# Attention starts straight from the projections; router, expert weights and expert tiles go between its turns

## The reference, cut to what matters

```
xn  = layernorm(x)
q, k, v = xn@Wq * mod, xn@Wk * mod, xn@Wv      # 16 heads of width 8, mod = cos(phase)*amplitude
s   = q@k.T / sqrt(8) * cos(2*pi*(i-j)/2048)   # per head, 2048 x 2048
w   = softmax(s);  w = (w + roll(w, 1)) / sqrt(2)
att = (w@v) * mod, all heads side by side, @ Wo
# experts: 8, each token takes its two best
logits = small per-token attention of xn@wqkv.T (8x8, with its own exp)
top two logits -> two experts and two weights (softmax of the two)
he  = (silu(xn@w1[e,:352].T) * (xn@w1[e,352:].T)) @ w2[e].T
out = x + att + sum over the two experts of weight*he
```

## Time and profile before

| | us |
|---|---|
| median of 3 runs | 709.84 (708.99 to 710.26) |
| the profiled execution | 707.88 |
| its span, first to last instruction | 706.1 |
| attention, first score matmul to last value matmul | about 206.8 to 692.0 |
| mean granted TensorE clock | 0.962 |

### The profile page before, as it was taken

One profiled execution on the slowest core, in us unless ns is written; L12 is line 12 of the kernel. 1 busy time (PEld: TensorE's weight loads), 2 busy tenths in 40 slices (PEclk: granted clock), 3 DMA queues, 4 the chain that ended last, 5 costly groups with the idle time before them and its releaser, 6 DMA issues.

```text
span 706.1 us, 11470 instructions
## 1 busy us (share of the span) xinstructions
PE 621.4 (88%) x4151; PEld 201.4 (29%) x4152; DVE 220.7 (31%) x462; ACT 550.1 (78%) x530; POOL 93.3 (13%) x109
## 2 busy tenths in 40 slices
PE   3984057999989999999999999999999999999995
PEld 3841034677751111111111111111111111111113
DVE  7578024334420031423233142331414232005003
ACT  1466024233358999999999999999999999999992
POOL 2038720111110101010010101101010000000000
PEclk9998568899998999999999999999999999999999
DMA  4934321111141101011010101101010010000002
GB/s 129 313 121 148 120 62 66 45 45 59 48 131 47 43 5 46 16 31 36 12 46 1 47 16 31 43 3 46 1 46 25 19 35 1 3 1 1 1 0 63
DMA packets 33828, 34.44 MB, mean 49 GB/s; under 512 B 6092, under 2 KB 27878, under 8 KB 33650
## 3 DMA queue, kind: packets, MB, share of 16 engines
q1 hardware_dynamic: 30786, 27.01, 13.3%
q0 software_dynamic: 2992, 6.76, 2.9%
HBM read 21.14 MB, written 12.58 MB: 48 GB/s over the span
## 4 chain that ended last, share of the span: by engine, by line
PE 60%; ACT 18%; issue 13%; DVE 7%; SPq 2%; DMA 0%; ACTq 0%; DVEq 0%
PE ps L1098 23%; ACT big L581 16%; PE ps L1081 15%; PE ps L981 4%; PE ps L974 4%; PE ps L986 3%; DVE m L771 2%; PE ps L964 2%; SPq L339 2%; PE ps L1116 2%; PE ps L1105 1%; PE ps L915 1%; PE ps L906 1%; DVE big L717 1%; PE ps L959 1%
## 5 line engine op out<-in xcount | busy, mean ns | idle before, releaser
L581 ACT ACTIVATE big<-ps 128x1536 f32<-128x1536 f32 x342 | 471.2, 1459 | 11.9 <-PE ps L1081 4.5
L1098 PE MATMUL ps<-big,vh 128*32 128x512 f32 x2048 | 274.1, 607 | 0.1
L1081 PE MATMUL ps<-qa,ka 49*128 49x512 f16 x896 | 179.8, 385 | 12.2 <-ACT big L581 9.2
L771 DVE TENSOR_REDUCE m<-ps 128x1 f32<-128x512 f32 x128 | 88.5, 692 | 157.5 <-PE ps L1116 157.5
L1081 PEld LDWEIGHTS ps<-qa,ka 49*128 49x128 f16 x896 | 33.1, 93 | 227.1 <-ACT big L581 157.1
L1098 PEld LDWEIGHTS ps<-big,vh 128*32 128x32 f32 x2048 | 40.4, 108 | 103.8 <-issue 98.2
L436 POOL COPY vh<-vaug 128x144 f32 x16 | 5.1, 319 | 382.1 <-PE ps L1098 380.8
L1116 PE MATMUL ps<-ka,attnT 49*128 49x512 f16 x128 | 48.0, 375 | 6.0 <-DVE m L771 5.7
L755 DVE COPY osb<-ps 128x512 f32<-128x512 f32 x16 | 11.1, 692 | 126.7 <-PE ps L1098 126.7
L738 DVE TENSOR_TENSOR cs<-pair,ps 128x352 f32<-128x352 f32 x39 | 20.3, 521 | 85.2 <-PE ps L986 81.6
L553 ACT COPY y<-ps 128x128 f32<-128x128 f32 x39 | 10.4, 266 | 45.6 <-PE ps L974 45.6
(11 more groups left out here) (165 smaller groups left out, 370.9 us busy)
## 6 DMA issues: line engine op xcount, KB each, us to landing
qk_parts<-store SPq DMA_DIRECT2D x16, 256.0 KB
qa<-qk_parts SPq DMA_DIRECT2D x28, 128.0 KB
slots_x<-vh SPq DMA_DIRECT2D x5, 512.0 KB, 9.1
cs<-slots_x SPq DMA_DIRECT2D x20, 128.0 KB, 2.3
slots_y<-y POOLq DMA_DIRECT2D x19, 128.0 KB, 2.7
store<-in_L_ffn_w SPq DMA_DIRECT2D x4, 512.0 KB, 6.6
ka<-qk_parts SPq DMA_DIRECT2D x32, 64.0 KB, 2.1
qa<-qk_parts SPq DMA_DIRECT2D x28, 64.0 KB
```

Of the source, the lines that this page charges most:

```text
L581: nc.scalar.activation(probs[:, first % PROBS:first % PROBS + n, :], ps[:, first % RING:first % RING + n, :], ACT.Exp, scale=ISQ8 / (OPERA ...
L771: nc.vector.tensor_reduce(m4[:, j // NC, j % NC:j % NC + 1], ps[:, O_BANKS[(p - 1) % 2], :], AX, ALU.max).then_inc(m_reduced, 1)
L1081: ins = nc.tensor.matmul(ps[:, n % RING, :], k[at:at + KQ, P * o:P * o + P], q[at:at + KQ, CW * c:CW * c + CW], start=True, stop=True, til ...
L1098: ins = nc.tensor.matmul(ps[32 * c:32 * c + 32, O_BANKS[p % 2], :], vh[:, p % 2, o + 8 * b, :], probs[:, n % PROBS, :], start=k == 0, stop ...
```

## The change

A **turn** is now one group of scores with what stands behind it in the same step of a list (`turns()`) that all engines walk. Heads 0 to 11 (768 score tiles) go in 384 turns of two tiles, in a ring of four PSUM banks (banks 4 and 5 are used by the other work); heads 12 to 15 go in threes as before. One quad of value matmuls comes in every second turn of two tiles.

- Before attention only norm, projections (with the values between them), squares, shifts and order of the heads are left. The phase and amplitude loads move to ACT's queue, three memsets to POOL, the raw expert weights are loaded behind the operands of the first two heads, xnT is also written to DRAM.
- Router: projection half before attention, half in turns 1 to 4; its exp on ACT behind turn 12; ranks at turn 24.
- Scatters: piece i waits for score group 30 + 2i, so the last for group 92; then `qe` is cleared.
- Expert weights: one of 24 blocks a turn from turn 26, copied by DVE.
- Expert tiles: 39 tiles of seven turns each, turns 96 to 368. Each tile's weights are first copied by DMA from `w1T`, `w2T` into one of four fixed places, three tiles ahead. `widen` now gives the hidden rows already turned; silu is made of exp(-a) on ACT (no table change) and an add, a reciprocal and two multiplications on DVE.
- Jobs of the exact maxima: 13 a head from head 3, in every turn of two, but not in steps 4 and 5 of an expert tile.

The core of the diff (w1T, w2T staging, router and prologue code left out where it is only moved):

```diff
+TURNS_A_TILE = 7
+EXPERTS_AT = 96
+WEIGHTS_AT = 26
+SCATTER_AT = 30
+FIRST_JOB_HEAD = 3
-JOBS_A_HEAD = 11
+JOBS_A_HEAD = 13
...
+        def turns():
+            w, j = 0, 0
+            for g in range(SCORE_GROUPS + 2):
+                m, step = expert_step(g)
+                job = None
+                if (w % QUADS >= JOB_QUAD and j < jobs_before(w // QUADS + 1) and step not in (4, 5)
+                        and (g < PAIRS or (g - j) % 2 == 0)):
+                    job = (w // QUADS, j)
+                    j += 1
+                ready = first_of(g - 1) if g >= 1 else 0
+                quads = range(w, max(w, min(ready // NC, H * QUADS)))
+                w = quads.stop
+                yield g, job, quads
...
 # gpsimd
+            for r in range(2):
+                for t in range(NT):
+                    if r == 0 and t == 6:
+                        pool.wait_ge(pv_done, QUADS)
+                        head_values(2)
+                    pool.wait_ge(score_ready, SCATTER_AT + 2 * (r * NT + t))
+                    nc.gpsimd.indirect_dma_start(slots_x, bass.IndirectOffsetOnAxis(ap=slot[:, r, t:t + 1], axis=0),
+                                                 xn[:, t, :], None).then_inc(scattered, 16)
...
 # scalar
+            def decay_of(m):
+                act.wait_ge(a_ready, m + 1)
+                after(act, hidT_ready, m - 1)
+                nc.scalar.activation(decay[:, m % 2, :], ps[:, 4, 0:FP], ACT.Exp, scale=-1.0).then_inc(decay_ready, 1)
             for g in range(SCORE_GROUPS):
                 weights(g)
+                m, step = expert_step(g)
+                if step == 3:
+                    decay_of(m)
...
 # vector
+            def hidden(m):
+                k = m % 2
+                dve.wait_ge(decay_ready, m + 1)
+                then(nc.vector.tensor_scalar(decay[:, k, :], decay[:, k, :], 1.0, BIGGEST, ALU.add, ALU.min))
+                then(nc.vector.reciprocal(decay[:, k, :], decay[:, k, :]))
+                dve.wait_ge(a_ready, m + 1)
+                then(nc.vector.tensor_tensor(decay[:, k, :], decay[:, k, :], ps[:, 4, 0:FP], ALU.mult))
+                dve.wait_ge(g_ready, m + 1)
+                after(dve, y_ready, m - 1)
+                nc.vector.tensor_tensor(hidT[:, k, :, :].rearrange("p f s -> p (f s)"), decay[:, k, :], ps[:, 5, 0:FP],
+                                        ALU.mult).then_inc(hidT_ready, 1)
...
+            for g, job, quads in turns():
+                if job is not None:
+                    take_max(*job)
+                for w in quads:
...
+                if step == 0:
+                    rows_out(m)
+                if step == 3:
+                    hidden(m)
+                if step == 6:
+                    result_out(m)
...
 # tensor
+            def widen(m, b, ready):
+                pe.wait_ge(staged_ld[m % STAGES], (m // STAGES + 1) * 32)
+                pe.wait_ge(xgT_ready, m + 1)
+                after(pe, hidT_ready, m)
+                if b == 1:
+                    after(pe, y_copied, m)
+                for f, (f0, n) in enumerate(FCH):
+                    ins = nc.tensor.matmul(ps[0:n, 4 + b, P * f:P * f + P],
+                                           w1_of[m % STAGES][:, F * b + f0:F * b + f0 + n],
+                                           xgT[:, m % 2, :], start=True, stop=True)
+                ins.then_inc(ready, 1)
+            def result(m):
+                pe.wait_ge(hidT_ready, m + 1)
+                after(pe, y_copied, m)
+                for f, (f0, n) in enumerate(FCH):
+                    ins = nc.tensor.matmul(ps[:, 5, FP:FP + DM], hidT[0:n, m % 2, f, :],
+                                           w2_of[m % STAGES][0:n, f, :], start=f == 0, stop=f == NF - 1)
                 ins.then_inc(y_ready, 1)
+            def expert_work(g):
+                m, step = expert_step(g)
+                if step == 0:
+                    turn_rows(m)
+                elif step == 2:
+                    widen(m, 0, a_ready)
+                elif step == 3:
+                    widen(m, 1, g_ready)
+                elif step == 6:
+                    result(m)
...
-            for g in range(SCORE_GROUPS + 2):
+            for g, job, quads in turns():
                 if g < SCORE_GROUPS:
                     scores(g)
-                if w % QUADS >= JOB_QUAD and j < jobs_before(w // QUADS + 1) and (g - j) % 2 == 0:
-                    max_job(w // QUADS, j)
-                    j += 1
-                while w < H * QUADS and tiles_of_quad(w)[-1] < (g - 1) * GROUP_OF:
+                if job is not None:
+                    max_job(*job)
+                for w in quads:
                     weighted_values(w)
                     between(w)
-                    w += 1
+                if g == RANK_TURN:
+                    rank_tokens()
+                if weight_block(g) is not None:
+                    turn_weights(weight_block(g))
+                expert_work(g)
```

More of the change, by code:

```diff
@@ L944, in _ @@
-            for n in range(16):
-                i, c = n // NC, n % NC
-                g, which = i // 2, i % 2
-                if n >= 4:
-                    pe.wait_ge(rot_ready, n - 3)
-                for half in range(2):
-                    ins = nc.tensor.matmul(ps[64 * half:64 * half + 64, PROJ_BANKS[n % 4], :], wmat[:, which, 64 * g:64 * g + 64],
-                                           xnT[:, CW * c:CW * c + CW], start=True, stop=True, tile_position=(0, 64 * half))
-                ins.then_inc(proj_ps, 1)
@@ L1035, in _, with mix_tokens @@
-            for n in range(TILES - 2, TILES):
-                result(n, n, owners[n % GROUP])
-            pe.wait_ge(silu_ready, TILES)
-            pe.wait_ge(hid_ready, TILES)
-            pe.wait_ge(hidT_ready, TILES)
-            pe.wait_ge(y_copied, TILES)
+            def mix_tokens(t):
+                ins = nc.tensor.matmul(ps[:, 5, 3 * E * t:3 * E * t + 3 * E], xnT[:, P * t:P * t + P], wqkvT[:], start=True, stop=True)
+                if t == NT - 1:
+                    ins.then_inc(mix_ps, 1)
@@ new lines, in _ @@
+            pe.wait_ge(wmat_ld, 4 * 16)
+            turn_x(0)
+            turn_x(1)
+            pe.wait_ge(wqkv_ready, 1)
+            rotate(0)
+            turn_x(2)
+            rotate(1)
+            turn_x(3)
+            rotate(2)
+            rotate(3)
+            t = 0
+            for n in range(4, 16):
+                rotate(n)
+                for _ in range(1 if n % 3 else 2):
+                    values(t)
+                    t += 1
+            pe.wait_ge(norm_parts, 4)
+            pe.wait_ge(kmean_ready, 2)
@@ new lines, in _, with turn_rows @@
+            ins.then_inc(other_ps, 1)
+            pe.wait_ge(peak_ready, 1)
+            nc.tensor.matmul(ps[0:1, 3, 0:H], peak[:], ident[0:H, 0:H], start=True, stop=True).then_inc(peak_ps, 1)
+            for t in range(MIX_BEFORE):
+                mix_tokens(t)
+            def turn_rows(m):
+                pe.wait_ge(xg_ld[m // 2 % 2], m // 4 * 16 + 16)
+                after(pe, xgT_ready, m)
+                if m == 0:
+                    pe.wait_ge(wT_ready, E * NF)
+                nc.tensor.transpose(ps[:, 4, FP:FP + P], xg[:, m % 4, :], ident[:]).then_inc(xgT_ps, 1)
```

724 lines of the change are left out of this document (350 added, 374 removed).

## The result

The changed kernel takes 801.37 us (median of 4 runs, 799.14 to 802.67) against 709.84: a ratio of 1.129 (95% interval 1.126 to 1.132), 12.9% slower. The profiled execution took 800.3 us with a span of 798.5, and the prediction's sum is held against it. The side was right; the time lies 50 us above the forecast of 750 and 15 above the end of the range.

A forecast was written before the change was run, and what follows sets the result against it. ACT paces plain turns; in expert tiles PE stands 1.8 us for the chain through ACT and DVE. Start and twelve heads 616, four heads in threes 118, tail and outside 16 gave 750 us, range 690 to 785.

The forecast's parts named there:

- The clock falls in the stalls: Rival: half of the expert tiles run their 5 us behind the stall at 1.2 GHz, 98 us more, 848; chance 0.05.
- start of attention: Work ahead of the first scores: attention begins at 61 us instead of 206.8, bounds 56 and 70.
- turns 0 to 95, stop at 96: Turns before the expert tiles: 29, 31 and 43 us, and 4 around turn 96.
- 39 tiles: Expert tiles of seven turns each: 11.05 us a tile, 431 us in all, bounds 394 and 464.
- turns 369 to 383: Two-tile turns behind the last expert tile: 15 us, with jobs 17.
- four heads in threes: Last four heads, in groups of three tiles: 115 us, and 3 for change of rings and eleven jobs, 118.
- tail and outside: End of the kernel: tail of 14 us as before and 2 outside the span, 16.
- The stall at full clock: Expert tile, step 6: PE stands 1.8 us before the result, waiting for hidden rows; tile 11.05 us.
- The reciprocal: DVE's reciprocal of 384 columns in the expert tile's chain: 6.25 ns a column, 2.55 us.
- The jobs' waits: Expert tiles: jobs wait for DVE's reduction, 0.66 us in some 0.6 of the tiles, 0.4 us a tile.
- The rival in which the chain fits: Rival: PE never stands in expert tiles, 8.9 us each, 347 us for 39, 666 in all; chance 0.20.
- The early start: Attention starting at 61 us instead of 206.8: a gain of 146 us at the start.

The follow-up runs named there:

- run 2: Changed kernel with six matmuls of zeros on PE ahead of the result in 36 of 39 tiles; 774.1 us in one execution, a second took 1238.54.
- run 6: Changed kernel with the reciprocal on only half of the 384 columns (silu wrong in the others); 729.16 us, ratio 1.029.
- run 8: Run 3's kernel plus 32 transposes before the first scores and jobs from head 4, 15 a head; 699.97 us, ratio 0.987.
- run 9: Run 8's kernel with 56 transposes and jobs kept apart by a quad or expert products; 687.71 us, ratio 0.968.
- run 1: Changed kernel with a multiplication by a constant in place of the reciprocal, so silu is not computed; 708.12 us, ratio 1.000.
- run 3: Changed kernel with silu by tanh on ACT and a shorter DVE chain without reciprocal, same function; 708.58 us, ratio 1.000.
- eight-turn forms: Kernels with eight turns an expert tile, tiles from turn 68: with the reciprocal 764.2 us, with jobs moved too 723.77; with tanh 693.36.
- run 5: Changed kernel with each result moved to step 1 of the next tile, no jobs in steps 4 to 6, jobs from quad 3; 763.59 us.
- run 12: Changed kernel with eight turns a tile from turn 68, tanh, 56 transposes, jobs kept apart in any step; 693.36 us, ratio 0.977.
- run 11: Changed kernel, reciprocal kept, eight turns a tile from turn 68, jobs apart and outside steps 4 to 6, 56 transposes; 723.77 us, ratio 1.021.

## Why the prediction was right in its side and wrong in its size

**The step that failed is "The clock falls in the stalls",** which I put among the rivals with a chance of 0.05 and left out of the likeliest sum. I had read the earlier trace rows as: 3.23 us lowers the clock, less does not. But the row with the shorter stalls had none that came back every tile, and absence of a row between 0 and 3.23 us was no evidence for the end I chose. Such a row did stand in the trace of the kernel before, at the start of its attention, where no stall is longer than 1.65 us (PE alone):

```profile
206.00:208.00 2.00, 0.97 (x8) 1.00 0.69 217
208.00:210.00 2.00, 0.73 (x3) 0.65 0.16 53
210.00:212.00 2.00, 1.69 (x8) 0.50 0.60 154
...
209.27 1.03 PE L1081 MATMUL ps<-qa,ka 49*128 49x512 f16 x3 [1.65 <-ACT big L581]
```

Runs 2 and 6 show that the fall is real and is worth 26 us: filled, 36 tiles keep the clock at 11.23 us; with the stall cut to mostly under 0.75 us, 37 keep it. As a price 98 was too much: it had half of the tiles losing 5 us each; it was 13 of 38, each 13.36 - 11.23 = 2.13 us. The clock's part is 28 of the missing 50 us in the tiles; the rest is spread over the other terms of the sum.

The sum, stage by stage (starts from the timelines of the changed kernel; what stands under "of it" sums up to the difference only roughly):

| stage | predicted us | measured us | of it |
|---|---|---|---|
| start of attention | 61 | 66.0 | first operands land later |
| turns 0 to 95, stop at 96 | 107 | 109.1 | half clock for 12 us at the start |
| 39 tiles | 431 | 466.1 | 13 x 2.13 = 28 by the clock, 38 x 0.18 = 7 in the full-clock tile |
| turns 369 to 383 | 17 | 22.3 | clock 0.62 for 9 us behind the last tile |
| four heads in threes | 118 | 120.5 | |
| tail and outside | 16 | 16.3 | |

```profile
66.00:78.00 12.00, 11.96 (x52) 5.03 (x56) 3.38 (x4) 6.56 (x7) 0.00 (x0) 0.50 0.70 175
...
641.00:650.00 9.00, 7.98 (x38) 1.38 (x40) 3.06 (x5) 4.59 (x5) 0.00 (x0) 0.62 0.02 7
```

- *The stall at full clock: right.* Predicted 11.05 us a tile, measured 11.23; stall predicted 1.8, mostly 1.36 to 1.95.
- *The reciprocal: right.* 2.55 us from the line through the earlier trace rows, 2553 ns measured. The repeat count of 8 in the Trainium skill ("VectorE: DVE Perf Modes", "First, the fixed hardware budget"), taken as eight cycles a column, would have been 3.2 us by my estimate; the trace does not bear that reading out.
- *The jobs' waits: there, at half their price.* I had 0.66 us in 0.6 of the tiles, 0.4 a tile. The trace has 19 waits for reductions, 8.4 us in all or 0.22 a tile: seven of them are of 0.66 us, most others of 0.29. Runs 8 and 9 bear them out, where the waits fell from 13.1 to 4.8 us.
- *The rival in which the chain fits* was priced at 666 us. Runs 1 and 3 are that case, and give 708: PE's own tile is 9.48, not 8.9; 39 x 0.58 = 23. The jobs' waits, which I had left out of it, are 0.23 of the 0.58 (8.9 us in run 1); the rest is not taken apart. The second tile's stop for the exact operands is 8 more, the late start 5, and 666 + 36 is 702; the last 6 stay open. So what would have been a gain of 44 us is nearly none: without the chain the change is a draw.
- *The early start*, worth 140 us (206.8 to 66.0), was had nearly as predicted. The scatters' pace was rightly given no price.

Not settled: why 13 tiles lose the clock and 25 with like stalls do not, why the first operands came 5 us later than in the sum, and what ACT's waits in the eight-turn forms are due to.

## What to carry to other kernels

When work is threaded between the turns of a stream that keeps PE full, the longest chain from one PE result through another engine back to PE must be shorter than PE's own work between the two places; count it from the rows before choosing the places, and ask of each repair what else queues on the engine that runs the chain. Price a recurring PE stall by its length and by the clock behind it, and test the second by filling the stall with idle matmuls. Before moving a function to DVE to save ACT a table load, look for a form of it that ACT has in the table already loaded: here tanh took the place of the reciprocal and 93 us with it.

## What the runs showed of the hardware that I had not expected

- A PE stall of 1.5 to 2 us in every 11 lowers the granted clock behind it in a third of the tiles; with stalls of mostly under 0.75 us 37 of 38 tiles kept it (run 6), and the last one had a stop of 2.7 us. In run 5 all four stalls of 1.8 to 1.9 us were followed by a lowered clock and three of ten of 1.1 to 1.2 us.
- One pause of 1.66 us behind transposes at 0.97 of the clock was followed by some 10 us at half, though PE was busy 3.93 and 4.00 of 4 us in that time (run 9): coming back took several times longer than the pause. With 0.86 us the same happened (run 12), with 0.29 us it did not (run 11).
- Reciprocal on DVE costs 2553 ns for 384 fp32 columns, against 554 for a product with a PSUM operand and 359 for a tensor-scalar.
